# A mixture-of-experts layer on one core: register loads moved behind the row transposes, 111 units for 112, a unit's scatter issued when it is weighed

## The chip, the cores and the metric

The kernel runs on one core of a Trainium2 chip. The metric is the device time of one execution in microseconds; the median of three runs before the change is 2360.02 us (2355.07 to 2368.59). Lower is better.

## The reference

Input `x` has 4 x 512 tokens of width 512. A cross attention and a causal self attention with 16 heads come first. What the change touches is the last stage, a mixture of experts over all T = 2048 tokens (16 experts, 6 per token, inner width 352) beside a shared expert of inner width 704:

```python
h = rmsnorm(x, ln2_w); t = h.reshape(-1, d)
probs = softmax(t @ gate_w.T)
topv, topi = top_k(probs, 6); topv = topv / sum(topv)
cw = zeros((T, 16)).at[arange(T)[:, None], topi].add(topv)
g = einsum('td,eid->eti', t, eg_w)
u = einsum('td,eid->eti', t, eu_w)
hh = silu(g) * u
routed = einsum('eti,edi,te->td', hh, ed_w, cw)
shared = (silu(t @ sg_w.T) * (t @ su_w.T)) @ sd_w.T
out = x + routed + shared
```

All arithmetic is of float32 precision: every product is made of three matmuls on values split in a high and a low part (`matmul3`, lines 58 to 62: high by high at L60, high by low at L61, low by high at L62).

## The kernel before

Four stages run one after the other: cross attention, self attention, norm and gate logits, shared expert. The shared expert stage also sorts the chosen (token, expert) pairs by expert and packs them into **units** of 128 rows of one expert each. `UNITS` (line 41) is the most that can be needed, rounded up to an even number: 112. For each unit, tables in SBUF hold its tokens (`token_of`), their weights (`weight_of`), its expert (`expert_of`) and where in the ring that expert's weights lie (`base_of`). Rows that stay empty point to a spare row. The tables of experts and bases are computed in two halves of `HALF` units.

The routed loop (`routed_experts`) then handles the units in order. A ring in SBUF has three slots (`SLOTS`), each for the weights of one expert in high and low halves (two DMAs of 2176 KB). For a unit n:

1. POOL gathers the unit's 128 rows from DRAM into `xg[n % 2]` by an indirect DMA (L1347).
2. TensorE transposes them (`transposed`, L1396, four transposes; the "row transposes"), ACT copies the high part (L1450), DVE makes the low part (L1475).
3. TensorE makes the gate and the up product (24 matmuls of 352 columns), ACT the silu (L1455), DVE the product `prod` (L1497).
4. TensorE transposes `prod` (L1431, three transposes), ACT and DVE split it (L1459, L1503).
5. TensorE makes the down product (nine matmuls of 512 columns, `down`), DVE multiplies by the weights (`weigh`, L1482) into `y[n % 2]`.
6. POOL scatters `y` with addition into the output in DRAM by an indirect DMA (L1351). Scatters follow each other strictly: each waits until those before it have landed (`added`), since two units may hold the same token.

TensorE's order in `step(n)` is: gate and up of n, row transposes of n+1, down of n-1, transposes of `prod` of n. All engines turn in hardware loops of two units (`Fori`), so the places of weights in the ring come from registers: `base(n)` and the expert are loaded by `value_load` (L1400, L1417; the profile shows a TENSOR_LOAD on the sequencer of TensorE, named PEldq). In the loops a wait compares with a register, and `ring[:, bass.ds(at + ..., size)]` costs the sequencer a register operation for most matmuls. The sequencer works ahead of TensorE's array.

POOL's order in `step(n)` is: wait for the indices of the step (`dve_i`) and for the row transposes of n (`pe_x`), gather of n+2, wait for the weighing of n-2 and the landing of the scatters before, scatter of n-2. DVE copies the indices of both at the start of its step (`indices`). POOL's `carry` additions (L1358) only take semaphore waits.

SP fills the ring: experts 1 and 2 at once, expert e from 3 to 15 when the last unit of expert e-3 has had its down product (`pe_d`), and in order behind the load before. The DMAs of SP are in one queue (q1), POOL's gathers and scatters in another (q0); both run on the same 16 DMA engines.

## Time and profile before

| | before |
|---|---|
| median of 3 runs | 2360.02 us |
| profiled execution, its own time | 2356.88 us |
| its span, first to last instruction | 2355.1 us |
| TensorE matmuls busy | 2198.8 us, 93% |
| TensorE weight loads busy | 1902.2 us, 81% |
| DVE, ACT, POOL busy | 51%, 29%, 42% |
| mean granted TensorE clock | 0.974 |
| q1 (SP), q0 (POOL), share of 16 DMA engines | 28.9%, 13.0% |
| gather L1347, scatter L1351: mean time on POOL | 1.06, 1.59 us |
| gather, scatter: median from issue to landing | 3.9, 4.7 us |

How to read it. The profiler lists instructions by engine with start, length and the source line. PE is TensorE's matmul, PEld its weight load, a q behind an engine's name its sequencer. "Idle before" in brackets is the time that the engine had stood still, with what ended it: an instruction of another engine, a DMA, or "issue", when nothing that the profile shows was waited for. The time "to landing" of a DMA runs from its issue until the last of its 16 parts has counted up its semaphore. The routed loop runs from about 1534 us to the end; the execution's own time includes 1.8 us around the span.

### The profile page before, as it was taken

How to read it: one execution, taken by the hardware profiler on the slowest of the kernel's cores; microseconds unless marked ns; L12 is line 12 of the kernel's file. 1: busy time of each engine (PE TensorE's matmuls, PEld its weight loads, DVE VectorE, ACT ScalarE, POOL GpSimd, SP SyncE). 2: the span in 40 equal slices, each digit the busy share in tenths (PEclk: the TensorE clock that was granted, in tenths of full speed). 3: DMA queues.
4: the chain of work that ended last, by engine and by line, in shares of the span. 5: the costliest groups of instructions: out<-in, count | busy, mean ns of one | idle time of the engine just before them, and what ended most of it. 6: DMA issues, size and time to landing. Idle time of an engine off the chain costs nothing. (4 is left out here: it accounts for less than half of the span.)

```text
span 2355.1 us, 40339 instructions
## 1 busy us (share of the span) xinstructions
PE 2198.8 (93%) x12102; PEld 1902.2 (81%) x12103; DVE 1210.0 (51%) x2735; ACT 691.8 (29%) x1612; POOL 983.7 (42%) x1047
## 2 busy tenths in 40 slices
PE   6889999999999999999967889889999999999996
PEld 4678888989888888888856667678888889888886
DVE  5736656464656566565655776623333333333332
ACT  5623334343433334333333111012222222222221
POOL 1225454545535454445443033334444344434442
PEclk9889999999999999999979999999999999999999
DMA  3113343443434333434445011265656665666433
GB/s 134 54 45 122 133 148 116 152 142 120 169 111 151 125 137 126 152 120 143 160 167 191 1 63 45 79 207 154 213 154 194 175 151 154 165 203 156 76 71 54
DMA packets 113401, 308.10 MB, mean 131 GB/s; under 512 B 13776, under 2 KB 13776, under 8 KB 107216
## 3 DMA queue, kind: packets, MB, share of 16 engines
q1 hardware_dynamic: 87888, 248.32, 28.9%
q0 software_dynamic: 25184, 58.74, 13.0%
q8 instruction: 22, 0.36, 0.1%
q10 hardware_dynamic: 288, 0.53, 0.1%
q14 instruction: 19, 0.16, 0.0%
HBM read 181.18 MB, written 126.35 MB: 131 GB/s over the span
## 5 line engine op out<-in xcount | busy, mean ns | idle before, releaser
L544 POOL TENSOR_TENSOR chunk_hi<-chunk_raw,zero 128x512 fp32r<-128x512 f32 x160 | 166.4, 1040 | 251.2 <-DMA chunk_raw<-in_whole 251.2
L1497 DVE TENSOR_TENSOR prod<-ps,silu 128x352 f32<-128x352 f32 x112 | 58.7, 524 | 311.4 <-PE ps L62 311.3
L546 POOL TENSOR_TENSOR chunk_raw<-chunk_raw,chunk_hi 128x512 fp32r<-128x512 f32 x160 | 206.6, 1291 | 12.6
L1358 POOL TENSOR_TENSOR carry<-ident 128x1 f32<-128x1 f32 x220 | 55.3, 251 | 362.7 <-DVE gidx L1490 216.6
L733 DVE TENSOR_TENSOR pT_lo<-ps,pT_hi 128x512 fp32r<-128x512 f32 (+3 forms) x256 | 119.6, 488 | 166.6 <-ACT pT_hi L679 166.6
L1351 POOL DMA_INDIRECT out<-y,sidx x112 | 178.1, 1590 | 64.3 <-issue 40.3
L707 DVE SCALAR_TENSOR_TENSOR HS<-ps,rinv,HS 128x512 f32<-128x512 f32 x260 | 176.4, 738 | 1.2 <-PE ps L62 1.2
L673 ACT ACTIVATE prob<-ps,negmax 128x512 f32<-128x512 f32 (+3 forms) x256 | 131.5, 526 | 112.0 <-DVE negmax L696 112.0
L60 PE MATMUL ps<-ring,xT_0hi 128*128 x448 | 151.3, 338 | 12.7 <-issue 8.9
L1482 DVE TENSOR_SCALAR y<-ps,weight_of 128x512 f32<-128x512 f32 x112 | 84.1, 751 | 142.2 <-PE ps L62 84.0
L60 PE MATMUL ps<-ring,xT_1hi 128*128 x448 | 149.8, 334 | 5.2 <-issue 3.8
L60 PE MATMUL ps<-wv_or_qk_hi,hT_hi 128*128 128x256 f32 x512 | 146.2, 286 | 8.3 <-POOL wv_or_qk_lo L539 8.3
L60 PE MATMUL ps<-ring,hT_hi 128*128 x336 | 141.9, 422 | 6.2 <-issue 4.2
L61 PE MATMUL ps<-wv_or_qk_lo,hT_hi 128*128 128x256 f32 x512 | 146.0, 285 | 0.0
L62 PE MATMUL ps<-wv_or_qk_hi,hT_lo 128*128 128x256 f32 x512 | 146.0, 285 | 0.0
L62 PE MATMUL ps<-ring,xT_0lo 128*128 x448 | 145.2, 324 | 0.0
L61 PE MATMUL ps<-ring,xT_0hi 128*128 x448 | 144.8, 323 | 0.0
L62 PE MATMUL ps<-ring,xT_1lo 128*128 x448 | 144.4, 322 | 0.0
L659 ACT ACTIVATE qkT_hi<-ps 128x512 fp32r<-128x512 f32 x128 | 76.6, 598 | 229.3 <-PE ps L62 229.3
L61 PE MATMUL ps<-ring,xT_1hi 128*128 x448 | 143.9, 321 | 0.0
L1045 POOL TENSOR_SCALAR in_lane<-count,xg 128x128 fp32r<-128x128 f32 x96 | 62.1, 661 | 183.0 <-PE ps L1064 91.6
L1347 POOL DMA_INDIRECT xg<-normed_rows,gidx x110 | 116.4, 1059 | 47.1 <-issue 42.4
(291 smaller groups left out, 6305.1 us busy)
## 6 DMA issues: line engine op xcount, KB each, us to landing
ring<-split_weights SPq DMA_DIRECT2D x31, 2176.0 KB, 11.4
chunk_raw<-in_whole SPq DMA_DIRECT2D x162, 256.0 KB, 2.7
split_weights<-chunk_hi SPq DMA_DIRECT2D x160, 256.0 KB, 2.4
split_weights<-chunk_raw SPq DMA_DIRECT2D x160, 256.0 KB, 2.6
xg<-in_wqk SPq DMA_DIRECT2D x17, 512.0 KB, 3.4
xg<-in_wv SPq DMA_DIRECT2D x9, 512.0 KB, 3.4
x<-in_x SPq DMA_DIRECT2D x4, 1024.0 KB, 5.7
x_spill<-x SPq DMA_DIRECT2D x4, 1024.0 KB, 3.9
```

The source lines that it names most:

```text
L60: nc.tensor.matmul(out, lhs[0], rhs[0], start=start, stop=False)
L61: nc.tensor.matmul(out, lhs[0], rhs[1], start=False, stop=False)
L62: return nc.tensor.matmul(out, lhs[1], rhs[0], start=False, stop=stop)
L544: nc.gpsimd.tensor_tensor(chunk_hi[k][:], chunk_raw[k][:], zero[:].to_broadcast([P, CH]), ALU.add).then_inc(chunk_high, 1)
L546: nc.gpsimd.tensor_tensor(chunk_raw[k][:].bitcast(F32R), chunk_raw[k][:], chunk_hi[k][:].bitcast(F32), ALU.subtract).then_inc(chunk_low, 1)
L659: nc.scalar.mul(qkT[0][:, m, :], ps_p[m][:], SCALE if m == 0 else 1.0).then_inc(act_qk, 1)
L673: nc.scalar.activation(prob[i][:], ps_s[i][:, 0:(i + 1) * P], ACT.Exp, bias=negmax[:, s % 2, i:i + 1], accum_out=rsum[:, s % 2, i:i + 1]). ...
L707: nc.vector.scalar_tensor_tensor(out=hs, in0=ps_w[i][:], scalar=rinv[:, (s - 1) % 2, i:i + 1], in1=hs, op0=ALU.mult, op1=ALU.add).then_inc ...
L733: nc.vector.tensor_tensor(pT[1][:, 0:i + 1, w], ps_t[k % 2][:, 0:(i + 1) * P].rearrange("p (j t) -> p j t", t=P), pT[0][:, 0:i + 1, w].bit ...
L1347: nc.gpsimd.indirect_dma_start(xg[q][:, 0, :], None, rows, bass.IndirectOffsetOnAxis(ap=gidx[q][:], axis=0), bounds_check=T + P - 1, oob_i ...
L1351: nc.gpsimd.indirect_dma_start(out, bass.IndirectOffsetOnAxis(ap=sidx[q][:], axis=0), y[q][:], None, bounds_check=T + P - 1, oob_is_err=Tr ...
L1482: nc.vector.tensor_scalar(y[q][:], ps_d[q][:], weight_of[:, bass.ds(n, 1)], None, ALU.mult).then_inc(dve_y, 1)
```

## The change

The three parts are: in TensorE's program the register loads for the gate products of the next unit move between the row transposes and the down products, where that of the down products is, and the loop is turned so that a step ends with the gate products of unit n+1; `UNITS` is 111, without rounding up, and the tables' second half overlaps the first by a unit; on POOL, step n scatters unit n-1 in place of n-2, and DVE copies the scatter's indices just ahead of the weighing.

```diff
@@ -38,7 +38,7 @@
 NSH = 2
 NE = E + NSH
 IT = [(0, 128), (128, 128), (256, 96)]
-UNITS = ((T * TOPK + E * (P - 1)) // P + 1) // 2 * 2
+UNITS = (T * TOPK + E * (P - 1)) // P
 GU, DN = 2 * DC * I, len(IT) * D
 EW = GU + DN
 WARM = EW + GU
@@ -928,7 +928,7 @@
-    HALF = UNITS // 2
+    HALF = (UNITS + 1) // 2
@@ -1187,7 +1187,7 @@
-                    of_unit = slice(half * HALF, (half + 1) * HALF)
+                    of_unit = slice(half * (UNITS - HALF), half * (UNITS - HALF) + HALF)
@@ -1306,7 +1306,8 @@
 
     NI = len(IT)
     LOADED = 48
-    TURNS = UNITS // 2 - 1
+    TURNS = (UNITS - 3) // 2
+    assert UNITS == 2 * TURNS + 3
     FIRST = 16 * begin.shape[-1]
     with ExitStack() as ctx:
         sb = lambda name, shape, dt=F32: ctx.enter_context(nc.sbuf_tensor(name, shape, dt))
@@ -1357,20 +1358,19 @@
                 pool.wait_ge(pool_c, ONE + done)
                 nc.gpsimd.tensor_tensor(carry[:], ident[:, 0:1], ident[:, 0:1], ALU.add).then_inc(pool_c, 1)
 
-            def step(n, q, first=False, more=True):
-                pool.wait_ge(dve_i, ONE + n + 1)
-                if more:
+            def step(n, q, scatters=True, gathers=True):
+                if gathers:
+                    pool.wait_ge(dve_i, ONE + n + 1)
                     pool.wait_ge(pe_x, ONE + n + 1)
                     take_waits(2 * n)
                     gather(q)
-                if not first:
-                    pool.wait_ge(dve_y, ONE + n - 1)
-                    pool.wait_ge(added, FIRST + 16 * (n - 2))
-                    if more:
-                        take_waits(2 * n + 1)
-                    scatter(q)
-                elif more:
+                if scatters:
+                    pool.wait_ge(dve_y, ONE + n)
+                    pool.wait_ge(added, FIRST + 16 * (n - 1))
+                if gathers:
                     take_waits(2 * n + 1)
+                if scatters:
+                    scatter(1 - q)
 
             for counter in counters:
                 nc.gpsimd.sem_inc(counter, ONE)
@@ -1379,14 +1379,13 @@
             pool.wait_ge(pool_0, 2)
             pool.wait_ge(added, FIRST)
             for n in range(2):
-                step(n, n, first=True)
+                step(n, n, scatters=n > 0)
             with pool.Fori(1, TURNS) as g:
                 for q in range(2):
                     step(2 * g + q, q)
-            for n in range(2 * TURNS, UNITS + 2):
-                step(n, n % 2, more=False)
+            for n in range(2 * TURNS, UNITS + 1):
+                step(n, n % 2, gathers=n + 2 < UNITS)
             pool.wait_ge(added, FIRST + 16 * UNITS)
-            pool.wait_ge(ld_x[1], 16 * (UNITS // 2))
 
         @block.tensor
         def _(pe):
@@ -1402,9 +1401,8 @@
             def weights(at, columns, size):
                 return [ring[:, bass.ds(at + (half * EW + columns), size)] for half in range(2)]
 
-            def down(n, q, weighed):
-
-                at = base(n)
+            def down(at, n, q, weighed=True):
+
                 if weighed:
                     pe.wait_ge(dve_y, ONE + n - 1)
                 pe.wait_ge(dve_h, ONE + n + 1)
@@ -1412,9 +1410,10 @@
                     last = matmul3(nc, ps_d[q][:], [h[:, c, :] for h in hT], weights(at, GU + c * D, D), c == 0, c == NI - 1)
                 last.then_inc(pe_d, 1)
 
-            def step(n, turn, q, before=2, more=True):
-                at = base(n)
-                expert = pe.value_load(expert_of[0:1, bass.ds(n, 1)], min_val=0, max_val=E - 1)
+            def expert(n):
+                return pe.value_load(expert_of[0:1, bass.ds(n, 1)], min_val=0, max_val=E - 1)
+
+            def gate_up(at, expert, n, q):
                 pe.wait_ge(ld_ring, 32 * expert + LOADED)
                 pe.wait_ge(dve_x, ONE + n + 1)
                 for m, (bank, done) in enumerate(((ps_g, pe_g), (ps_u, pe_u))):
@@ -1422,25 +1421,38 @@
                         last = matmul3(nc, bank[:, 0:I], [x[:, j, :] for x in xT[q]], weights(at, (m * DC + j) * I, I),
                                        j == 0, j == DC - 1)
                     last.then_inc(done, 1)
-                if more:
-                    transposed(turn + 1 + q, 1 - q)
-                if before:
-                    down(n - 1, 1 - q, before > 1)
+
+            def products(n):
                 pe.wait_ge(dve_p, ONE + n + 1)
                 for c in range(NI):
                     last = nc.tensor.transpose(ps_h[:, c * P:(c + 1) * P], prod[:, c * P:(c + 1) * P], ident[:])
                 last.then_inc(pe_h, 1)
 
+            def step(n, turn, q, before=2):
+                transposed(turn + 1 + q, 1 - q)
+                if before:
+                    previous = base(n - 1)
+                following, its_expert = base(n + 1), expert(n + 1)
+                if before:
+                    down(previous, n - 1, 1 - q, before > 1)
+                products(n)
+                gate_up(following, its_expert, n + 1, 1 - q)
+
             pe.wait_ge(pool_0, 2)
+            first, its_expert = base(0), expert(0)
             transposed(1, 0)
-            step(0, 0, 0, before=0)
-            step(1, 0, 1, before=1)
+            gate_up(first, its_expert, 0, 0)
+            for n in range(2):
+                step(n, 0, n, before=n)
             with pe.Fori(1, TURNS) as g:
                 for q in range(2):
                     step(2 * g + q, g, q)
-            step(2 * TURNS, TURNS, 0)
-            step(2 * TURNS + 1, TURNS, 1, more=False)
-            down(UNITS - 1, 1, True)
+            for q in range(2):
+                step(2 * TURNS + q, TURNS, q)
+            previous, last = base(UNITS - 2), base(UNITS - 1)
+            down(previous, UNITS - 2, 1)
+            products(UNITS - 1)
+            down(last, UNITS - 1, 0)
 
         @block.scalar
         def _(act):
@@ -1465,8 +1477,8 @@
             with act.Fori(1, TURNS) as g:
                 for q in range(2):
                     step(2 * g + q, q)
-            step(2 * TURNS, 0)
-            step(2 * TURNS + 1, 1, more=False)
+            for n in range(2 * TURNS, UNITS):
+                step(n, n % 2, more=n + 1 < UNITS)
 
         @block.vector
         def _(dve):
@@ -1478,20 +1490,13 @@
             def weigh(n, q):
 
                 dve.wait_ge(added, FIRST + 16 * (n - 1))
+                nc.vector.tensor_copy(sidx[q][:], token_of[:, bass.ds(n, 1)])
                 dve.wait_ge(pe_d, ONE + n + 1)
                 nc.vector.tensor_scalar(y[q][:], ps_d[q][:], weight_of[:, bass.ds(n, 1)], None, ALU.mult).then_inc(dve_y, 1)
 
-            def indices(n, q, scatters=True, gathers=True):
-
-                if scatters:
-                    dve.wait_ge(added, FIRST + 16 * (n - 3))
-                    last = nc.vector.tensor_copy(sidx[q][:], token_of[:, bass.ds(n - 2, 1)])
+            def step(n, q, before=True, gathers=True, more=True):
                 if gathers:
-                    last = nc.vector.tensor_copy(gidx[q][:], token_of[:, bass.ds(n + 2, 1)])
-                last.then_inc(dve_i, 1)
-
-            def step(n, q, before=2, gathers=True, more=True):
-                indices(n, q, before > 1, gathers)
+                    nc.vector.tensor_copy(gidx[q][:], token_of[:, bass.ds(n + 2, 1)]).then_inc(dve_i, 1)
                 dve.wait_ge(act_s, ONE + n + 1)
                 dve.wait_ge(pe_u, ONE + n + 1)
                 nc.vector.tensor_tensor(prod[:, 0:I], ps_u[:, 0:I], silu[:], ALU.mult).then_inc(dve_p, 1)
@@ -1507,15 +1512,13 @@
             dve.wait_ge(added, FIRST)
             low_rows(0, 0)
             for n in range(2):
-                step(n, n, before=n)
+                step(n, n, before=n > 0)
             with dve.Fori(1, TURNS) as g:
                 for q in range(2):
                     step(2 * g + q, q)
-            step(2 * TURNS, 0, gathers=False)
-            step(2 * TURNS + 1, 1, gathers=False, more=False)
-            indices(UNITS, 0, gathers=False)
-            weigh(UNITS - 1, 1)
-            indices(UNITS + 1, 1, gathers=False)
+            for n in range(2 * TURNS, UNITS):
+                step(n, n % 2, gathers=n + 2 < UNITS, more=n + 1 < UNITS)
+            weigh(UNITS - 1, (UNITS - 1) % 2)
 
 
 def program(nc, x, ctxT, wqkT, bqk, ln1, ln2, wqk, wv, wo, gateT, whole, out):
```

## Rows read from the trace of the kernel before

**Rows 1.** The chain of waits, 1530 to 2356 us: start us, length us, what.
```profile
1556.43 0.66 PE ps L1396 x4
...
1714.38 0.44 PE ps L1396 x4
...
1721.04 0.44 PE ps L1396 x4
...
1733.00 9.08 DMA xg<-normed_rows,gidx
...
2326.52 0.44 PE ps L1396 x4
```

**Rows 2.** Waits, 1545 to 2340 us: total us, times, longest.
```profile
PEld ps L60 <- issue: 42.5, 87, 1.6
```

**Rows 3.** Source view of L1417, whole run: ns min/median/max, first and last start.
```profile
L1417 PEldq TENSOR_LOAD <-expert_of x112: 295/302/1002, 1534.6 to 2327.9; - x112
```

**Rows 4.** Timeline, 2203 to 2211 us: start, us, engine, line [idle before].
```profile
2204.26 0.69 DVE L1475 TENSOR_TENSOR xT_0lo<-ps,xT_0hi 128x512 fp32r<-128x512 f32 x1 [0.46 <-ACT xT_0hi L1450]
...
2206.45 0.43 PE L60 MATMUL ps<-ring,xT_0hi 128*128 x1 [0.44 <-issue]
...
2210.29 0.41 PEld L1396 LDWEIGHTS ps<-ident,xg 128*128 128x128 f32 x3
```

**Rows 5.** Source view of L1400, 2204 to 2209.3 us.
```profile
L1400 PEldq TENSOR_LOAD <-base_of x2: 297/299/301, 2204.3 to 2208.7; - x2
```

**Rows 6.** Source view of L1341, 1730.5 to 1731.3 us.
```profile
L1341 SPq DMA_DIRECT2D ring<-split_weights x2: 327/382/438, 1730.6 to 1731.0; - x2
...
DMA to landing us min/median/max: 10.2/13.2/16.3
```

**Rows 7.** Timeline, 1731 to 1750 us.
```profile
1731.97 0.14 DVE L1490 COPY gidx<-token_of 128x1 uint32 x1
...
1734.44 1.60 POOL L1351 DMA_INDIRECT out<-y,sidx  x1 [0.16 <-issue]
...
1734.64 0.60 PE L1396 MATMUL ps<-ident,xg 128*128 128x128 f32 x4
...
1742.13 0.66 PE L1396 MATMUL ps<-ident,xg 128*128 128x128 f32 x4 [0.34 <-DMA xg<-normed_rows,gidx]
...
1743.20 0.50 PE L60 MATMUL ps<-ring,hT_hi 128*128 x1 [0.41 <-issue]
...
1749.64 0.60 PE L1396 MATMUL ps<-ident,xg 128*128 128x128 f32 x4
```

**Rows 8.** Source view of L1347, 1560 to 2340 us.
```profile
DMA to landing us min/median/max: 3.3/3.9/9.1
```

**Rows 9.** Source view of L1351, 1734 to 1735 us.
```profile
DMA to landing us min/median/max: 13.0/13.0/13.0
```

**Rows 10.** Timeline, 2339 to 2356 us.
```profile
2339.41 0.75 DVE L1482 TENSOR_SCALAR y<-ps,weight_of 128x512 f32<-128x512 f32 x1 [2.65 <-PE ps L62]
...
2342.95 1.54 POOL L1351 DMA_INDIRECT out<-y,sidx  x1 [3.87 <-DMA out<-y,sidx]
```

**Rows 11.** Source view of L1351, 1869 to 1870 us.
```profile
L1351 POOL DMA_INDIRECT out<-y,sidx x1: 1591/1591/1591, 1869.6 to 1869.6; - x1
...
DMA to landing us min/median/max: 14.1/14.1/14.1
```

**Rows 12.** Source view of L1347 (gathers), 1874.5 to 1876 us.
```profile
L1347 POOL DMA_INDIRECT xg<-normed_rows,gidx x1: 1060/1060/1060, 1875.1 to 1875.1; - x1
...
DMA to landing us min/median/max: 9.1/9.1/9.1
```

**Rows 13.** Source view of L1351 (scatters), 1650 to 1651 us.
```profile
DMA to landing us min/median/max: 10.7/10.7/10.7
```

**Rows 14.** Timeline, 1254 to 1256 us.
```profile
1254.57 0.51 PE L60 MATMUL ps<-hT_hi,gate_hi 128*128 128x512 f32 x1 [4.06 <-DVE hT_lo L915]
```

**Rows 15.** Busy us by engine, granted clock (PEclk), DMA share, GB/s.
```profile
1255.30:1258.70 3.40, 3.40 (x10) 2.66 (x9) 3.40 (x3) 0.00 (x0) 3.40 (x3) 0.50 0.00 0
```

## The prediction

> **What bounds the kernel now.** Read the busy shares and the granted clock first, then the chain of waits through the routed loop, then its waits, then single units and one event on the timeline, then the landings of the DMAs. TensorE is 93% busy, and the routed loop, the part that the diff touches, is a chain of its products. What the reader is to see is how far its units lie from the shortest. The row transposes of L1396 come once per unit: from the set at 1556.43 to the last there are 108 steps in 770.1 us, 7.13 us each, while an undisturbed step takes 1721.04 - 1714.38 = 6.66 us [rows 1]. So some 51 us of the loop are not products. They have two causes.
>
> The first is the register loads, three a unit: base and expert ahead of the gate and up products, base again ahead of the down products. The weight loader waits for "issue" ahead of L60 for 42.5 us in 87 places [rows 2]. An expert load takes 0.30 us at the median and up to 1.00 us [rows 3]. In one unit the base load starts at 2204.3, the expert load follows, and the next gate products begin at 2206.45, 0.44 us after TensorE had run dry [rows 4, 5].
>
> The second is the transfers, once per expert. SP sends the next expert's weights (two DMAs of 2176 KB) when the last unit of an old expert is through; with 16 experts and three slots that happens 13 times. The weights that go out at 1730.6 and 1731.0 land 10.2 and 16.3 us after their issues [rows 6]. POOL's gather of 1733.00 comes just in time for the transposes at 1742.13, which had waited 0.34 us for it: 9.1 us, where the shortest gather takes 3.3 [rows 1, 7, 8]. The scatter of 1734.44 needs 13.0 us [rows 9]. The down products start at 1743.20, after 0.41 us of waiting for one register load; the next transposes at 1749.64 [rows 7].
>
> **The change part by part.**
>
> *Register loads behind the transposes.* All three now stand between the row transposes of unit n+1 and the down products of n-1, so the gate products of n+1 find their registers ready. What the place costs: today's base load there starts at 2208.7, TensorE comes to the transposes at 2210.29 and to the down products 0.5 us later, so the sequencer is 2.1 us ahead [rows 4, 5]. From the base load of 2204.3 to the products of 2206.45 two loads, one of them slow, take 2.15 us [rows 4, 5]; with the slow one at 0.30 I estimate 0.75 us a load, 2.25 us for three: bare by 0.15. But the lead grows: the sequencer may go into the gate products when the low rows are split, at 2204.26 + 0.69 = 2204.95, 1.06 us before TensorE runs dry at 2206.01 [rows 4], not 0.44 behind it. I take 0 for a calm unit; the bounds are 0 and 0.85 us (0.15 and a load at its longest, 0.7 more). Gain: the 69 calm steps go to 6.66 us, 459.5 us.
>
> The Trainium skill ("Advanced Engine Details and Errata", Engine Queue Depths) gives TensorE's queue 64 instructions. The lead in the rows, 2.1 us, is ten products of 0.16 us and four transposes, each with its weight load, 28 instructions. By the page the lead has room to double; by the rows alone it may end there, and each calm unit keep 0.15 us, 10 us in all.
>
> What the loads lose is cover: after a late gather the sequencer stands at the transposes. Now one load follows bare (1742.13 to 1743.20, 1.07 us); then three will, 1.07 + 2 x 0.75 = 2.57 us.
>
> *The scatter, issued when weighed.* This part decides. Around an event POOL's order is today: gather of n+3, scatter of n-1, gather of n+4. It becomes scatter of n-1, gather of n+3. Weighing takes 0.75 us from the end of the down products [rows 10], which is also what sends the weights out; with some 0.9 us from a semaphore to the DMA instruction (the gather's index copy ends at 1731.97 + 0.14 = 1732.11, the gather goes at 1733.00 [rows 1, 7]) the scatter goes at +1.7 us from the weights' issue instead of +3.8. It holds POOL for 1.6 us [rows 7], so the gather goes at +3.7 instead of +2.4. POOL has time: both together take 1.6 + 1.06 of 6.66 us. In a calm unit the gather then lands at about +7.7 (3.9 at the median [rows 8]), the sequencer comes to its transposes at about +8 and TensorE at +10.5. Cost: 0; if the sequencer has to wait a little, the 0.9 us of the grown lead pays for it.
>
> In an event the cost is not the 1.3 us but the place in the queue, for gathers and scatters share one. The scatter of 1869.6 landed 14.1 us later, at 1883.7; the gather of 1875.1 behind it took 9.1 us and landed at 1884.2, half a microsecond after the scatter, though alone it needs 3.3 [rows 8, 11, 12]. And the scatter of 1734.44 landed at 1747.4, just after the second half of the weights (1731.0 + 16.3 = 1747.3) [rows 6, 7, 9]. So this queue and the weights take turns; what is first in the queue is through at +11.5, what is second only as the weights end. With the scatter in front, the gather that the transposes wait for lands where the scatter lands now: between +14.6 (10.7 us, an early event) and +18.1 (14.1 us) [rows 11, 13]. I take the middle, L = 16.3. Bound below: the later issue alone, +12.7.
>
> An event covers three steps, from transposes at +4.0 (1734.64) to the third set after. New length: L - 4.0, then 2.57 to the down products, 1749.64 - 1743.20 = 6.44 to the next transposes, and 6.66: L + 11.7 = 28.0 us, 13 times 363.6 us.
>
> *The clock.* TensorE then stands still from +10.6 to +16.3, and has only four transposes in the 2.6 us after that. The trace has a wait of 4.06 us before 1254.57, and from 0.7 us later a stretch of 3.4 us with granted 0.50 (1.2 of 2.4 GHz) in which TensorE is all busy [rows 14, 15]. In the routed loop the gaps are now of the size of 1 us and less and the profile's page shows full clock there. Cost 3.4 / 2 = 1.7 us an event, 22.1 us; bounds 0 and twice that.
>
> *111 units:* one step less, -6.7 us. *The tail:* the last scatter goes at 2342.95, after waiting for the one before, though its rows were weighed at 2339.41 + 0.75 = 2340.16 [rows 10]. The one before will have gone a unit earlier, so the last goes 0.9 us after weighing: -1.9 us. *At nothing:* the copy of the scatter's indices ahead of the weighing (0.14 us, where DVE waits for TensorE; without that cover 0.14 us a unit on DVE), the tables' middle unit made twice, the last wait for a gather dropped. Weighing will wait less for old scatters; TensorE hardly waits for that today.
>
> **Sum.** 459.5 + 363.6 + 22.1 = 845.2 us in place of 770.1: +75.1. With -6.7 and -1.9: +66.5. On the profiled execution's 2356.88 us (span 2355.1) that is 2423 us. The median of the runs is 3 us above the profiled one; I don't add it.
>
> **The rivals.**
>
> 1. *Faster: the scatter in front doesn't hold the gather up* (11%). Then L stays 11.5, an event is 23.2 us, 13 are 301.2, the loop 760.7; with unit and tail -18 us, 2339 us. The point from which it decides is L = 12.9, where gain and loss meet. For it: a gather that is first gets through an event in 9.1 us with half of the weights still to come. Against it: the landings of 1883.7 and 1884.2 [rows 11, 12]. The Trainium skill ("DMA: Bandwidth & Descriptors", Queues, rings and completion order) says that a DMA engine turns between queues by whole packets, typically 9 to 17 descriptors. By that the scatter and the gather would be gone in a turn or two, and this rival's 2339 us come out. The same section says that descriptors of one engine's ring are taken in order; the two landings agree.
> 2. *The same: only the issue moves* (6%). L = 12.7: 459.5 + 13 x 24.4 = 776, with -8.6 2354 us. For it, the gather's 9.1 us, which need no order in the queue; against it the same two landings.
> 3. *Slower by less* (12%): every event as quick as the early one, L = 14.6, and the clock holds: 459.5 + 13 x 26.3 = 801, with -8.6 +22, 2379 us. For it the 10.7 us.
> 4. *The loads bare in every unit too* (5%): 69 x 0.75 = 52 us on top of the sum, 2475 us. For it, a lead of 2.1 us against 2.25; against it, the lead that grows.
> That the change doesn't do what it says could only be rival 4; the swap on POOL is written out in its order.
>
> **How the numbers follow.** The forecast has 66%, from 2395 to 2450 us (L from 15 to 18, clock 0 to 3.4 us an event). With rivals 3 and 4 slower has 83%, the same 6%, faster 11%; 0.5%, 12 us, is about what a measurement of this kernel tells from none. The range for 8 in 10 is 2358 to 2450: below it rival 1 and part of 2, above it rival 4.
>
> **What would show it.** Right: hardly a wait for "issue" ahead of the gate products, calm steps of 6.7 us; a scatter 0.9 us after each weighing and the gather behind it; 13 waits of 4 to 7 us for a gather at the row transposes, of gathers that take 11 to 14 us; granted clock 0.50 after them; waits for "issue" of about 2 us ahead of the down products there. Wrong: gathers that land by +12.9 us in an event, or calm steps over 6.9 us.

## The result and the profile after

The changed kernel takes 2429.34 us (median of 4 runs, 2424.44 to 2435.02), the kernel before beside it 2359.15 us: a ratio of 1.0293, 95% interval [1.0254, 1.0331], slower. The profiled execution took 2424.44 us. The forecast of 2423 us and its main mechanism held. Several of its terms did not, and the experiments show which.

The page of the changed kernel: the span, two rows of busy shares, the granted clock in 40 slices, the chain by engine.

```profile
span 2422.5 us, 40216 instructions
PE 2208.2 (91%) x12062; PEld 1918.8 (79%) x12063; DVE 1208.3 (50%) x2729; ACT 690.8 (29%) x1609; POOL 985.2 (41%) x1043
...
PE   6889999999999999999859788799888889988997
...
PEclk9889999999999999999979899899989999999999
```

TensorE has 40 matmuls fewer and yet is 9 us longer busy. In slices 29 to 39, all nines before, the PE row now has seven eights, and the clock row has eights at slices 23, 26 and 30 that were not there. Slice 23 lies ahead of the routed loop.

The waits between 1545 and 2340 us (total us, times, longest):

```profile
POOL carry L1359 <- DMA out<-y,sidx: 122.3, 13, 9.7
...
PE ps L1395 <- DMA xg<-normed_rows,gidx: 58.8, 13, 5.7
...
PEld ps L60 <- issue: 29.9, 20, 2.4
PE ps L60 <- issue: 23.1, 18, 2.1
```

The wait for "issue" of [rows 2] fell from 87 places to 20, and where it is left it is long: it now stands mostly ahead of the down products of an event. New are 13 waits of the row transposes for a gather.

One event on the timeline, where SP, POOL, DVE and PE rows answer to [rows 7]. The weights go out at 1844.15 us.

```profile
1844.15 0.91 SPq L1342 DMA_DIRECT2D ring<-split_weights  x2
```

```profile
1844.25 0.75 DVE L1495 TENSOR_SCALAR y<-ps,weight_of 128x512 f32<-128x512 f32 x1 [0.80 <-PE ps L62]
```

```profile
1846.04 1.60 POOL L1352 DMA_INDIRECT out<-y,sidx  x1 [0.59 <-DVE gidx L1499]
1847.14 0.72 POOL L1359 TENSOR_TENSOR carry<-ident 128x1 f32<-128x1 f32 x1
1848.02 1.07 POOL L1348 DMA_INDIRECT xg<-normed_rows,gidx  x1 [0.15 <-issue]
1858.46 0.18 POOL L1359 TENSOR_TENSOR carry<-ident 128x1 f32<-128x1 f32 x1 [9.37 <-DMA out<-y,sidx]
```

```profile
1848.11 0.60 PE L1395 MATMUL ps<-ident,xg 128*128 128x128 f32 x4
...
1859.62 1.11 PE L1395 MATMUL ps<-ident,xg 128*128 128x128 f32 x4 [4.67 <-DMA xg<-normed_rows,gidx]
...
1871.40 0.60 PE L1395 MATMUL ps<-ident,xg 128*128 128x128 f32 x4
```

The chain of waits through the same event: the gather's flight, and the loads behind it.

```profile
1848.02 11.56 DMA xg<-normed_rows,gidx
...
1860.74 1.60 issue
1862.34 0.79 PE ps L60
```

The scatter goes 1.04 us after its rows are weighed (1844.25 + 0.75 = 1845.00), the gather 2.0 us behind it. The scatter lands 12.3 us after its issue, at 1858.3, the second half of the weights at 1859.3, the gather at 1859.6, which is 15.4 us after the weights' issue. In all 13 events the gather lands 0.2 to 0.5 us behind the second half of the weights. Then three loads stand bare: 2.72 us from the transposes to the down products.

The clock around it (columns: window, its length, busy PE, PEld, DVE, ACT, POOL, granted clock, DMA share, GB/s):

```profile
1850.00:1856.00 6.00, 4.95 (x31) 4.49 (x29) 2.01 (x6) 0.94 (x2) 0.00 (x0) 1.00 1.02 382
1856.50:1857.80 1.30, 0.00 (x0) 0.00 (x0) 0.00 (x0) 0.00 (x0) 0.00 (x0) 1.00 0.84 340
1857.90:1868.10 10.20, 6.88 (x20) 5.50 (x21) 1.87 (x4) 1.07 (x2) 3.25 (x5) 0.50 0.34 73
```

TensorE stood still from 1854.95 (1859.62 less 4.67), and from 1857.9 the granted clock is 0.50, 1.2 of 2.4 GHz, for 10.2 us. All 13 events have such a stretch. It is 6.8 us long in the seven in which the transposes waited 3.8 to 4.2 us for the gather, and 10.2 us in the six in which they waited 4.7 to 5.7.

**The loop as a sum.** From the transposes at 1554.84 to the last set at 2394.44 there are 107 steps in 839.6 us, where the forecast has 845.2 - 6.7 = 838.5:

```profile
1554.84 0.60 PE L1395 MATMUL ps<-ident,xg 128*128 128x128 f32 x4
```

```profile
2387.77 0.60 PE L1395 MATMUL ps<-ident,xg 128*128 128x128 f32 x4
2394.44 0.60 PE L1395 MATMUL ps<-ident,xg 128*128 128x128 f32 x4
```

A calm step is 2394.44 - 2387.77 = 6.67 us. 68 of them are 453.6 us, which leaves 386.0 for 13 events, 29.7 us each; forecast were 28.0 + 1.7 = 29.7. Counted by their own transposes, though, the events' three steps take 27.7 to 31.4 us, 29.3 in the mean. Most of the other 5 us lie in the loop's first step, 10.65 us from 1554.84. It is a 14th event, which the forecast did not count: expert 2's weights went at 1543.3, the gather of 1545.39 lands at 1554.5, just in time, and 2.1 us of bare loads and 3.4 us at half clock follow.

**The tail.** The last rows are weighed at 2407.48 + 0.75 = 2408.23, and the last scatter goes 2.0 us later, again after a wait for the one before; before the change it was 2342.95 - 2340.16 = 2.8 us [rows 10]. So the tail brought 0.8 us, not 1.9.

```profile
2410.23 1.54 POOL L1352 DMA_INDIRECT out<-y,sidx  x1 [3.76 <-DMA out<-y,sidx]
```

```profile
2407.48 0.75 DVE L1495 TENSOR_SCALAR y<-ps,weight_of 128x512 f32<-128x512 f32 x1 [2.64 <-PE ps L62]
```

### The profile page after: what moved, and what is told of

Its sections match the earlier page's. It is cut to its first block and busy times, and to the rows that moved or that the text cites. A ratio compares the mean times of both kernels' runs of the same rounds, so it can differ in the third digit from the quotient of the medians.

```text
span 2422.5 us, 40216 instructions
## 1 busy us (share of the span) xinstructions
PE 2208.2 (91%) x12062; PEld 1918.8 (79%) x12063; DVE 1208.3 (50%) x2729; ACT 690.8 (29%) x1609; POOL 985.2 (41%) x1043
## 5 line engine op out<-in xcount | busy, mean ns | idle before, releaser
L1359 POOL TENSOR_TENSOR carry<-ident 128x1 f32<-128x1 f32 x218 | 97.6, 448 | 447.1 <-DVE y L1495 313.8
L546 POOL TENSOR_TENSOR chunk_raw<-chunk_raw,chunk_hi 128x512 fp32r<-128x512 f32 x160 | 206.8, 1292 | 12.6
L60 PE MATMUL ps<-ring,hT_hi 128*128 x333 | 151.4, 455 | 24.6 <-issue 23.1
L61 PE MATMUL ps<-ring,hT_hi 128*128 x333 | 139.6, 419 | 0.0
L62 PE MATMUL ps<-ring,hT_lo 128*128 x333 | 139.5, 419 | 0.0
```

What stands on the lines that cost most here:

```text
L60: nc.tensor.matmul(out, lhs[0], rhs[0], start=start, stop=False)
L61: nc.tensor.matmul(out, lhs[0], rhs[1], start=False, stop=False)
L62: return nc.tensor.matmul(out, lhs[1], rhs[0], start=False, stop=stop)
L546: nc.gpsimd.tensor_tensor(chunk_raw[k][:].bitcast(F32R), chunk_raw[k][:], chunk_hi[k][:].bitcast(F32), ALU.subtract).then_inc(chunk_low, 1)
L1359: nc.gpsimd.tensor_tensor(carry[:], ident[:, 0:1], ident[:, 0:1], ALU.add).then_inc(pool_c, 1)
```

## The experiments

### First set: which part, and what the collision is with

**e1: gather ahead of the scatter again.** The changed kernel with POOL's old order; the register loads and 111 units stay.

```diff
                 if scatters:
-                    pool.wait_ge(dve_y, ONE + n)
-                    pool.wait_ge(added, FIRST + 16 * (n - 1))
+                    pool.wait_ge(dve_y, ONE + n - 1)
+                    pool.wait_ge(added, FIRST + 16 * (n - 2))
...
-                    scatter(1 - q)
+                    scatter(q)
```

> The changed kernel, but POOL scatters unit n-2 behind the gather of n+2 again, as before the change; TensorE's order, the 111 units and DVE's order stay. Theory Q (the gather stands behind the scatter in POOL's DMA queue while the weights load): the gathers of the 13 events land 11.5 us after the weights' issue again, an event is 23 us, no half clock in the loop, calm steps 6.67 us: 2340 us, 2330 to 2350. Rival L (the three register loads, or the turned loop, are what made it slower): stays near 2429. Rival T (only the later issue of the gather counts): 2340 too; the next run but one tells T from Q.

Measured: 2358.66 us (10 runs), ratio to before 1.0003 [0.9981, 1.0026], above the expected range. Its waits:

```profile
PE ps L60 <- issue: 29.7, 25, 2.1
...
PE ps L1395 <- DMA xg<-normed_rows,gidx: 3.3, 9, 1.0
```

The gather waits went from 58.8 to 3.3 us and the time by some 70 us: POOL's order is the whole loss. But the gain of the two other parts did not show. The chain through one event says most of why: a gather that lands just in time (weights at 1596.2) still has the loads bare behind it, and the clock drops for a stretch after that, in nine of the 13 events. The rest lies outside the events: 12 of the 68 other steps are over 6.8 us again, in the changed kernel one.

```profile
1598.54 8.58 DMA xg<-normed_rows,gidx
...
1607.82 1.81 issue
```

```profile
1610.00:1613.40 3.40, 3.40 (x10) 2.52 (x9) 0.15 (x1) 0.00 (x0) 0.42 (x2) 0.51 0.52 164
```

**e2: POOL's new order on the old tensor program.** The kernel before, 112 units, its three loads where they were; POOL scatters n-1 and DVE copies the scatter's index ahead of the weighing.

```diff
-                    pool.wait_ge(dve_y, ONE + n - 1)
-                    pool.wait_ge(added, FIRST + 16 * (n - 2))
...
-                    scatter(q)
+                    pool.wait_ge(dve_y, ONE + n)
+                    pool.wait_ge(added, FIRST + 16 * (n - 1))
...
+                    scatter(1 - q)
...
```

> The kernel before with only the new order on POOL and DVE (scatter of n-1 in step n, its indices copied ahead of the weighing); TensorE's loads as before, 112 units. Theory Q: the 13 waits for a gather of 4 to 6 us are there, one register load bare behind each instead of three, calm steps 6.67 to 7.25 us as before: 2420 to 2440 us. Rival L: 2350 to 2365, as before.

Measured: 2407.92 us in one run, 50 us over the kernel before. 13 gather waits, and the bare loads of an event are gone, as the old place has one load there and not three:

```profile
PE ps L1395 <- DMA xg<-normed_rows,gidx: 53.8, 13, 5.1
PE ps L60 <- issue: 1.6, 4, 0.8
```

The kernel before, same window:

```profile
PE ps L60 <- issue: 16.9, 50, 0.7
```

Below the range that I expected. Two things were smaller than I took them for. No half-clock stretch is longer than 6.8 us: they are 82 us in all, for 109 in the changed kernel. And the waits of the calm units went too, 16.9 us down to 1.6, though no register load was moved; the steps outside the events take 6.85 us in the mean, for 7.05 before and 6.74 in the changed kernel. The starts of the loads show what it goes with. Between 1575 and 2340 us of the kernel before, 59 of 320 register loads take over 0.4 us, and 52 of the 59 start 1.9 to 2.9 us after POOL has issued a scatter. In e2 it is 11 loads, in the changed kernel 13, and all of them start in that same time after a scatter. With the scatter moved, fewer loads start there. Why a load is slow there is open.

**e3: the gather first, but later.** e1 with a 512-wide `carry` addition (1.03 us) ahead of the gather, which moves its issue from +2.35 to +2.85 us after the weights.

```diff
-                    take_waits(2 * n)
+                    take_waits(2 * n, 512)
                     gather(q)
```

> As the run with the gather first, but the additions that take POOL's waits ahead of each gather are 512 wide instead of 1, so that each gather is issued about 1 us later, still ahead of its scatter. Tells Q from T. Q: the gather keeps its place, its landing in an event moves by the delay at most, +12.5 us, 13 us on the run with the gather first: 2345 to 2358 us. T (the issue time counts, not the place; the changed kernel's is 1.4 us later than before): most of the loss is back, 2400 us or more.

Measured: 2379.2 us (5 runs), 1.0091 [1.0058, 1.0125], between the two expectations. 0.5 us of issue cost 1.2 us of landing (in the mean 12.2 us after the weights for 11.0) and 20 us of time: the moment of issue counts too, more than one for one.

**e4: light weights.** The changed kernel with the weights of experts 3 to 15 cut to an eighth of the columns; the output lacks them.

```diff
+                    size = EW if e < SLOTS else EW // 8
-                    sp.dma_start(ring[:, at:at + EW]...
+                    sp.dma_start(ring[:, at:at + size]...
```

> The changed kernel with only the first eighth of each weight transfer from expert 3 on (the rest of the weights is left out, so the output is of wrong weights); everything else the same. Q, and any theory in which the weights' transfer is what delays the gather: no waits for gathers over 1 us, no half clock in the loop, all steps 6.67 us, about 120 us less than the changed kernel: 2300 to 2315 us. If scatter and gather hold each other up without the weights: over 2350 us.

Measured: 2306.04 us in one run, no wait for a gather, no half clock but in the loop's first step (expert 2's weights are whole), and but for that step and one other all the loop's are 6.6 to 6.8 us, in events too. So the collision with the weights in flight costs the changed kernel some 120 us, in waits, bare loads and clock together; without it the kernel is 52 us faster than the one before with all its weights.

### Second set: place or moment, and the bare loads

**e10: gather first at the scatter's time.** As e3 with two wide additions: the gather goes at +3.95 us, as in the changed kernel, but ahead of the scatter of its step.

```diff
-                    take_waits(2 * n, 512)
+                    for k in range(2):
+                        take_waits(3 * n + k, 512)
                     gather(q)
...
```

> The order on POOL of the kernel before (gather of n+3, then scatter of n-1) with two wide additions ahead of the gather, so that the gather is issued about 3.9 us after the weights, as in the changed kernel, yet ahead of its scatter. Theory Q (the place behind the scatter in the queue is what makes the gather late): it lands by +13.5 us, waits for gathers at the row transposes about 25 to 35 us in all, time 2385 to 2405 us. Theory T (only the time of the issue matters; the 0.45 us of the run before cost 1.4 us of landing): it lands at about +15.3 us as in the changed kernel, waits about 55 to 60 us, time 2420 to 2430 us.

Measured: 2394.1 us (4 runs), 1.0135 [1.0095, 1.0175], inside what theory Q (the place in the queue) expects. One event; the weights go at 1645.46, the chain gives the gather's flight:

```profile
1644.19 1.60 POOL L1353 DMA_INDIRECT out<-y,sidx  x1 [0.17 <-issue]
1647.11 2.15 POOL L1360 TENSOR_TENSOR carry<-zeros 128x512 f32<-128x512 f32 x2 [1.32 <-DVE gidx L1502]
1649.41 1.06 POOL L1349 DMA_INDIRECT xg<-normed_rows,gidx  x1 [0.15 <-issue]
1655.03 0.18 POOL L1360 TENSOR_TENSOR carry<-zeros 128x1 f32<-128x1 f32 x1 [4.56 <-DMA out<-y,sidx]
```

```profile
1649.41 9.07 DMA xg<-normed_rows,gidx
```

Landing at +13.0 us, where the same issue time behind the scatter gave 15.3 in the mean. In all 13 events it lands ahead of the second half of the weights, in the changed kernel behind it. It is not a clean case, though: the scatter of 1644.19, issued 1.3 us ahead of the weights, was itself held up and landed at 1655, as in the other events, and the gather had to follow that one. Of the 70 us between e1 and the changed kernel, e10 has half.

**e7: the loads ahead of the transposes.** The changed kernel, one move; the sequencer then does its loads while it would wait for the gather anyway.

```diff
-                transposed(turn + 1 + q, 1 - q)
                 if before:
                     previous = base(n - 1)
                 following, its_expert = base(n + 1), expert(n + 1)
+                transposed(turn + 1 + q, 1 - q)
```

> The changed kernel with its three register loads put ahead of the row transposes in place of behind them; all else as it is. Theory (after a late gather three loads stand bare ahead of the down products, about 2 us more than needed in each of 13 events): the waits for issue ahead of the down products go, the 13 waits for gathers (about 60 us) and the half clock stay, calm steps 6.67 us, 2392 to 2408 us. Rival (the loads only looked bare; TensorE then waits for the same time elsewhere, or calm steps get longer because the loads lose the cover of the transposes): within 10 us of the changed kernel, 2420 to 2440 us.

Measured: 2394.35 us (4 runs), 1.0124 [1.0077, 1.0171], 35 us less than the changed kernel and inside the theory's range. The gather waits are as before (57.9 us in 13 places); no wait for "issue" ahead of the down products is left; the 13 half-clock stretches are 75 us in all instead of 109.

```profile
PE ps L1395 <- DMA xg<-normed_rows,gidx: 57.9, 13, 5.5
```

**e8: both.** e1 and e7 in one.

> Gather ahead of the scatter as on POOL before, and the loads ahead of the row transposes: the two places of an event mended at once. Theory (with the gather first, 2359 us; what was missing to the 2339 us of the blind rival are the bare loads and the half clock that they bring): nearly no wait for issue, little half clock, 2305 to 2325 us, about 2313. Rival (the half clock comes from the gather waits or from the load of weights itself and stays): about 2333 us.

Measured: 2343.14 us (5 runs), 0.9908 [0.9877, 0.994], 15 us less than e1, and over both expectations. The rival's mechanism is not it, for the half clock did go, except in 4 events of 13, and these 4 are a test of their own. The same kernel, the gather at the same +2.35 us after the weights, in one event of each kind (weights at 1680.12 and 1726.3):

```profile
1679.23 1.59 POOL L1352 DMA_INDIRECT out<-y,sidx  x1 [0.59 <-issue]
...
1682.47 1.06 POOL L1348 DMA_INDIRECT xg<-normed_rows,gidx  x1 [0.51 <-issue]
```

```profile
1728.65 1.06 POOL L1348 DMA_INDIRECT xg<-normed_rows,gidx  x1 [0.51 <-DMA out<-y,sidx]
```

```profile
1695.12 1.11 PE L1395 MATMUL ps<-ident,xg 128*128 128x128 f32 x4 [4.18 <-DMA xg<-normed_rows,gidx]
```

```profile
1737.47 0.65 PE L1395 MATMUL ps<-ident,xg 128*128 128x128 f32 x4 [0.34 <-DMA xg<-normed_rows,gidx]
```

In the first a scatter was issued 0.9 us before the weights and not yet through: the gather takes 12.3 us and TensorE waits 4.18. In the second the scatter before had landed: 8.6 us and 0.34. Neither the moment of issue nor the size of the weights differs; the scatter ahead in the queue is the difference. The first gather lands as the weights end, both at +14.7 us, the second at +10.9, with the weights at +16.5. All four events with such a scatter (issued from 0.9 us before the weights to 0.2 after) have waits near 4 us and a half-clock stretch; the nine others have no such stretch and wait 3.4 us together.

**e9: the early gather.** Scatter when weighed, the gather of n+3 issued a scatter earlier (in step n, behind the low rows of n+1), loads ahead.

```diff
-                    pool.wait_ge(dve_i, ONE + n + 1)
-                    pool.wait_ge(pe_x, ONE + n + 1)
+                    pool.wait_ge(dve_i, ONE + n + 2)
+                    pool.wait_ge(pe_x, ONE + n + 2)
-                    gather(q)
+                    gather(1 - q)
...
```

> Scatter when weighed, as in the changed kernel, but the gather of unit n+3 is issued in step n, right behind the low rows of n+1 that free its buffer, and not after the scatter of the next step; loads ahead of the transposes. Theory (the scatter does no harm where the gather that the next transposes need has gone before it): no waits for gathers over 1 us, no half clock, steps of 6.7 us also in events, 2305 to 2315 us. Rival (some gather still goes beside the weights and lands late, because each event covers more than a step): waits of 1 to 3 us in 13 places, 2325 to 2345 us.

Measured: 2331.71 us (4 runs), 0.9852 [0.9812, 0.9892]; the rival's range. Ten of the 13 events hardly wait; in the other three the scatter before had gone 0.8 to 0.9 us ahead of the weights, and the gather stood behind it after all: these three waits are 12.2 of the 13.2 us in 5 places.

### Third set: less in flight

**e11: the weights in pieces.** The changed kernel in its own order; each half in 4 DMAs of 544 KB, each issued when the one before has landed.

```diff
-                sp.wait_ge(ld_ring, LOADED + 32 * (e - 1))
                 for half in range(2):
-                    at = (e % SLOTS * 2 + half) * EW
...
+                    for piece in range(PIECES):
+                        sp.wait_ge(ld_ring, LOADED + 16 * (((e - 1) * 2 + half) * PIECES + piece))
+                        at = (e % SLOTS * 2 + half) * EW + piece * SIZE
...
-                pe.wait_ge(ld_ring, 32 * expert + LOADED)
+                pe.wait_ge(ld_ring, 32 * PIECES * expert + LOADED)
```

> The changed kernel with all its work, but each half of an expert's weights sent in 4 DMAs of 544 KB in place of one of 2176 KB, and each DMA issued only when the one before has landed, so that never more than 544 KB of weights stand beside a gather or a scatter. Theory (the cost of the change is the collision of the scatter and the gather behind it with 4.35 MB of weights in flight at once): no wait for a gather over 1 us, hence no bare loads and no half clock, steps of 6.7 us throughout, 2304 to 2318 us, about 2308. Rival (the total of the transfers counts, not how much is in flight; the weights now stand beside four or five units in place of two, and each of their gathers loses some time): waits of 0.5 to 2 us in 40 to 60 places, 2330 to 2400 us.

Measured: 2364.92 us (12 runs), 1.003 [1.0009, 1.0051]. Inside the rival's range, but without its waits: no row of PE waits for a gather at all, and yet 46 us are lost to "issue".

```profile
PEld ps L60 <- issue: 55.2, 38, 2.6
PE ps L60 <- issue: 46.3, 33, 2.4
```

The timeline of one such place:

```profile
1554.72 1.07 POOL L1352 DMA_INDIRECT xg<-normed_rows,gidx  x1 [0.16 <-issue]
```

```profile
1561.67 0.60 PE L1399 MATMUL ps<-ident,xg 128*128 128x128 f32 x4
...
1564.23 0.78 PE L60 MATMUL ps<-ring,hT_hi 128*128 x1 [1.96 <-issue]
```

That gather landed 6.5 us after its issue, 0.3 us ahead of the transposes: TensorE never waited for it, but its sequencer did, and lost its lead. Sorted by the time from the landing to the first weight load of the transposes (from the trace's semaphore events; the gap is that from the start of the last weight load of the row transposes to the start of the first of the down products, 0.11 us when nothing is late):

```
landing ahead of the transposes, us   gathers   mean gap, us
under 0.4                                  10           2.47
0.4 to 0.8                                  6           2.23
0.8 to 1.2                                 10           1.54
1.2 to 1.6                                  5           0.82
1.6 to 2.0                                  8           0.41
over 2.0                                   70           0.12
```

In the first five rows gap and lead add up to 2.1 to 2.9 us, about the time of three loads. A gather has to land 2 us before TensorE wants it, and where it doesn't, TensorE shows a wait for "issue" and none for the gather. In the changed kernel 49 gathers land 2.2 to 2.5 us ahead, just outside.

**e12: smaller pieces.** `PIECES = 8` in place of 4.

> As the run before with 8 DMAs of 272 KB for each half. Theory: as there, 2304 to 2318 us, no difference that can be told. Rival (16 DMAs one after the other take more than the 41 to 54 us between two experts, so that the weights fall behind and the gate products wait for them at the last experts): 2320 to 2380 us.

Measured: 2425.95 us (4 runs), 1.0288 [1.0243, 1.0333]. The theory's 2304 to 2318 fell; the rival's mechanism holds and costs more than it expected: one piece every 2.6 to 5.2 us, 16 pieces 51 to 56 us, more than the 41 to 54 that an expert's units take.

```profile
PE ps L60 <- DMA ring<-split_weights: 86.9, 14, 12.2
```

**e13: the kernel before with pieces.** The edit of e11 on the kernel before.

> The kernel before with the weights in the 4 pieces per half, so that the change can be valued without its collision: this against the changed kernel in pieces. From its own gaps of before: 110 steps of 6.66 us, waits for register loads of 35 to 40 us stay, the events lose their 1.8 us each (21.8 for 20.0 us, 13 of them, 23 us): 2356.9 - 23, 2325 to 2345 us, about 2334. So the change would make this kernel 20 to 30 us faster. Rival (events cost before nothing but loads; pieces bring nothing): 2350 to 2362 us.

Measured: 2354.4 us (10 runs), 0.9969 [0.9944, 0.9994]: the rival's range. The events' waits for gathers went (3.1 us before), but more time was lost to the loads ahead of the gate products, 21.1 us for 16.9. Loads over 0.4 us are 72 for 59, and all 72 start 1.9 to 2.9 us after a scatter's issue:

```profile
PE ps L60 <- issue: 21.1, 51, 0.8
```

The expected range was missed: the 20 to 30 us that the change was to bring here are not there. Against this run, e11 is 10 us slower: even with the weights in pieces the change alone doesn't pay.

**e14: pieces, and the loads ahead.** e11 with the move of e7.

> The changed kernel with the weights in 4 pieces per half and the three register loads ahead of the row transposes. Theory (in pieces no gather makes TensorE wait, but one that lands less than some 2 us before the transposes holds the sequencer there and so lays the loads behind it bare: 46 us in 33 places, and the half clock that follows): these go, what stays is 0.1 to 0.2 us a step of the loads ahead of the transposes, 2369 less 46, less 17 for ten half-clock stretches, plus 12 to 22: 2318 to 2328 us. Rival (in pieces the loads themselves are slower, or the gathers' lateness shows at the transposes once the loads no longer hide it): waits for gathers of 15 us and more, 2335 to 2350 us.

Measured: 2307.25 us (5 runs), 0.9793 [0.9767, 0.9819], the fastest that sends all the weights, and 51 us under the kernel before. Its waits, and a window of 720 us of its loop:

```profile
PEld ps L1399 <- issue: 13.3, 50, 0.4
```

```profile
1556.00:2276.00 720.00, 719.89 (x4253) 659.12 (x4252) 280.94 (x638) 162.85 (x319) 326.78 (x426) 1.00 0.69 165
```

TensorE is busy for 719.89 of 720 us at full granted clock. It beat my range of 2318 to 2328, which took the loads' wait of the weight loader ahead of the transposes (13.3 us) for lost time; PE itself lost nearly none.

## Why the prediction was right, and where it was not

*Calm units, 6.66 us: right, but not by the register loads alone.* 6.67 measured; the wait for "issue" ahead of the gate products is gone, and the lead grew enough. Rival 4 is out. The forecast gave this gain to the moved register loads. e2, which moves only the scatter, has the waits of TensorE for "issue" down from 16.9 to 1.6 us, and e1, which leaves the loads in their new place and takes the scatter back, has 12 long steps in 68 again: the scatter's new time kept the loads fast, which the forecast did not see.

*The scatter in front: right, the term that decides.* The scatter went 1.0 us after weighing (0.9 forecast), the gather at +3.8 to +3.9 (3.7). e1 takes this part back and with it the whole loss; e2 adds it alone and gets 50 us of loss. That the place in the queue does it, and not only the later issue, is shown by the two kinds of events in e8, at one issue time. e3 and e10 show that the issue time has a share of its own, but not how the 70 us divide: half are back in e10, whose gathers go late and also stand behind a late scatter. Rival 2 is out: it had landing at +12.7.

*L, mis-sized by 1 us.* 16.3 was forecast, the middle of 14.6 and 18.1; measured are 14.6 to 16.5, mean 15.3 us. The forecast put the gather where the scatter landed in the old order. The scatter now lands at 13.9 to 14.5, and the gather 0.6 to 2.0 us behind it, just after the second half of the weights. That the second in the queue is through as the weights end, as the forecast said, holds in all 13; but the weights now end at +14.1 to +16.3, mean 15.0, for +14.1 to +18.0, mean 16.0, before. Why they end earlier is not shown.

*The clock, mis-sized the other way.* I took one stretch of 3.4 us with half clock per event, 1.7 us. There were 6.8 or 10.2 us. The event's 29.3 us less L and the 11.67 of its other steps leave 2.3 us. So the misses are -1.0 and +0.6 us an event; with them go +4 us in the loop's first step and +1.1 in the tail. They nearly cancel, which is luck: the sum came closer than its terms deserve.

*The tail, mis-sized.* 1.9 us were forecast and 0.8 came, because the last scatter still waits for the one before (3.76 us, the row of 2410.23); the forecast had it go 0.9 us after weighing.

*Bare loads: right.* 2.57 forecast, 2.72 in the event shown; e7 gives back 35 us by moving them: the 23.1 us of TensorE's waits for "issue" are gone, and the half-clock stretches are 34 us shorter, worth up to 17.

*Rival 1's price, wrong.* I gave 2339 us for a gather that isn't held up. e1 is that case, with gathers at +11.0, and took 2358.66. The price had the bare loads in it (2.57 of the 23.2 us), but no clock. In e1 the clock fell after the bare loads in nine events, 3.4 us each, and an event takes 24.0 us. Some 10 us more are in the steps outside the events, 6.81 us in the mean for 6.66; 3.8 of them are the loop's first step. So gain and loss met at a landing of +11.0, not at L = 12.9, and e11's table says where the gain begins: at a landing about 2 us ahead of the transposes.

*Where the Trainium skill stands.* The turns that the prediction took from the Trainium skill ("DMA: Bandwidth & Descriptors", Queues, rings and completion order) can be checked in the packets of the event of 1844.15. From +6 to +14 us the trace has 147 packets of weights (17408 bytes, 0.66 us each) and 128 of the scatter (2048 bytes, 0.18 us), 17 to 24 of the one and 15 to 28 of the other in each full microsecond from +7 to +13. The scatter's come from +6.9 to +13.5; the gather's 64 come only from +13.2, as the scatter's end, and the last is through at +15.1. These counts fit engines that turn between the queues by one packet of each: 8 of either take 8 x (0.66 + 0.18) = 6.7 us, which is what the scatter's took. The Trainium skill's page has a whole packet of typically 9 to 17 descriptors to a turn, by which the scatter, 128 rows over 16 engines, would have been gone in a turn or two. Here the measurement decides against its use for rival 1, whether or not the profiler's packet is the skill's. The same section of the Trainium skill says that descriptors of a ring are taken in order, there for the queues of SP and ACT; the order of the packets agrees with it for POOL's queue too, and that is what holds the gather back. Turns do not explain that the scatter's first packet comes 5.0 us after its issue, for 2.2 us in the scatter after the event.

*Open.* The half-clock stretches go with the length of the wait in the changed kernel, but in e7, with waits of 3.9 to 5.5 us and no bare loads, they are 3.4 or 6.8 us in no such order. Nor is it settled why a scatter issued 1.5 us ahead of the weights lands at +4.0, one issued 1.3 ahead at +9 and one issued 0.8 ahead at +11.5 (e8, e10, e8), steps steeper than the issue.

## What to carry to other kernels

Before an operation is put ahead of another in a shared queue, ask what it will stand behind when the queue is slow, not how short it is in the calm case. A wait of the engine is not the only sign of a late input: the sequencer needs its own lead over the data (here 2 us for three register loads), and register loads belong ahead of the wait that may be late, not behind it. A big transfer can do less harm in a few pieces sent one by one, as long as the pieces keep up with their deadline: 2307 us for 2394 with the loads ahead (e14, e7), though only 2354 for 2361 in the kernel before (e13).

## What the runs showed of the hardware

- A register load is slow in the time after a scatter. In the changed kernel base loads take up to 0.74 us and expert loads up to 0.98, and between 1575 and 2340 us 13 of the 14 loads that start 1.9 to 2.9 us after a scatter's issue take over 0.4 us, none of the 276 others. With the loads ahead of the transposes (e7) none starts in that time, and none in the loop is over 0.32.

```profile
L1399 PEldq TENSOR_LOAD <-base_of x202: 295/303/741, 1546.2 to 2339.7; - x101
```

```profile
L1399 PEldq TENSOR_LOAD <-base_of x220: 294/303/322, 1546.2 to 2370.7; - x110
```

- A scatter of 128 rows lands 4.9 us after its issue at the median and up to 12.6 us beside 4.35 MB of weights; its own 256 KB are not what makes it slow.
- Behind a scatter a gather takes 4.1 to 7 us with at most 544 KB of weights in flight (e11, e14), and 10.7 to 12.6 us with 4.35 MB. Ahead of its scatter it takes 3.0 to 5.2 us (e13) and 8.2 to 9.4 us (e1).
- TensorE standing still for 2 us (bare loads in e1) was followed by 3.4 us at half clock in nine events of 13, about 4 to 5.7 us, with bare loads behind it, by 6.8 or 10.2.
